# Summing the scan's products by accumulating DMAs instead of GpSimd adds

## The reference

```python
def ffn(x):                                   # H = 512, I = 2048
    h = silu(x @ w_gate) * (x @ w_up)
    return keep_2_largest_of_4(h) @ w_down    # 2:4 sparsity by magnitude

def mamba(x):                                 # E = 1024 channels, N = 16 states
    xn = rmsnorm(x) * norm_w
    skip, u = xn @ W_skip.T, xn @ W_in.T
    u = silu(causal_conv4(u) + conv_b)
    delta = softplus(u @ Wd1.T @ Wd2.T + bd2)
    Bt, Ct, A = u @ WB.T, u @ WC.T, -exp(A_log)
    # for every token l, channel e, state n:
    #   h[e,n] = exp(delta[l,e] * A[e,n]) * h[e,n] + delta[l,e] * u[l,e] * Bt[l,n]
    #   y[l,e] = sum over n of h[e,n] * Ct[l,n]
    return ((y + u * W_D) * silu(skip)) @ W_out.T

x = x + 0.5 * ffn(layernorm(x))
x = x + mamba(layernorm(x))
x = x + 0.5 * ffn(layernorm(x))
```

## Time and profile before

| | |
|---|---|
| median of 3 runs | 4050.57 us (4049.12 to 4053.82) |
| profiled execution | 4051.71 us, its span 4050.0 us |
| PE busy | 3607.4 us (89%) |
| DVE busy | 3205.8 us (79%) |
| POOL busy | 2918.7 us (72%) |
| ACT busy | 2039.0 us (50%) |
| DMA queues of SP and ACT | 37.0% and 12.5% of the sixteen engines' span |

### The profile page before, as it was taken

How to read it: one execution, slowest core, us unless ns; L and a number is a source line. 1 busy time by engine, 2 the same in 40 slices (tenths; PEclk the granted TensorE clock), 3 DMA queues, 4 the chain that set the end, 5 groups by cost and what they waited for, 6 DMA issues and landing times. The chain is left out here.

```text
span 4050.0 us, 38161 instructions
## 1 busy us (share of the span) xinstructions
PE 3607.4 (89%) x11264; PEld 2077.2 (51%) x11264; DVE 3205.8 (79%) x3392; ACT 2039.0 (50%) x2694; POOL 2918.7 (72%) x2249
## 2 busy tenths in 40 slices
PE   7998889999999999899999898899887788787798
PEld 5654555555555555554555454545454344444455
DVE  4425988787989789887999889977988789989823
ACT  3234557547554664557554755466353665353310
POOL 0024789677977899688886998779967989878700
PEclk9999999999999999999999999999898898888899
DMA  6444545544645465354554555546454345444432
GB/s 234 148 134 140 162 147 168 201 148 148 211 159 182 146 202 191 120 187 154 201 172 154 173 164 188 155 139 202 156 171 133 124 148 180 148 126 148 122 123 90
DMA packets 233148, 647.64 MB, mean 160 GB/s; under 512 B 25968, under 2 KB 26224, under 8 KB 223216
## 3 DMA queue, kind: packets, MB, share of 16 engines
q1 hardware_dynamic: 159216, 510.95, 37.0%
q10 hardware_dynamic: 73728, 134.25, 12.5%
HBM read 579.57 MB, written 65.54 MB: 159 GB/s over the span
## 5 line engine op out<-in xcount | busy, mean ns | idle before, releaser
L1096 POOL TENSOR_TENSOR db<-du,Bb 128x512 f32<-128x512 f32 x1024 | 1357.5, 1326 | 539.8 <-DVE decay L990 459.9
L990 DVE TENSOR_TENSOR_SCAN decay<-decay,db 128x512 f32<-128x512 f32 x1024 | 1251.9, 1223 | 268.7 <-ACT decay L690 253.8
L1107 POOL TENSOR_TENSOR y<-y,pr 128x512 f32<-128x512 f32 x1024 | 1382.8, 1350 | 63.9 <-DVE pr L1000 63.9
L690 ACT ACTIVATE decay<-delta,aneg 128x512 f32<-128x512 f32 x1024 | 701.5, 691 | 1187.3 <-DVE pr L1000 1181.1
L523 PE MATMUL main<-zhi,wunit 128*128 128x512 f32 x2048 | 961.4, 469 | 54.4 <-DVE zlo L934 32.5
L582 PE MATMUL side<-h,wdown 128*128 128x512 f32 x2048 | 925.0, 595 | 16.1 <-DVE res_r L975 8.8
L524 PE MATMUL main<-zlo,wunit 128*128 128x512 f32 x2048 | 811.2, 396 | 0.0
L525 PE MATMUL main<-zhi,wunit 128*128 128x512 f32 x2048 | 809.8, 395 | 0.0
L1000 DVE TENSOR_TENSOR pr<-decay,Cb 128x512 f32<-128x512 f32 x1024 | 703.2, 687 | 31.5 <-DVE decay L990 0.3
L582 PEld LDWEIGHTS side<-h,wdown 128*128 128x128 f32 x2048 | 389.0, 190 | 425.6 <-issue 389.1
L598 PE MATMUL side<-xm,wmam 128*128 128x512 f32 x1024 | 488.4, 624 | 60.2 <-ACT cv L771 28.1
(11 more groups left out here) (80 smaller groups left out, 2624.2 us busy)
## 6 DMA issues: line engine op xcount, KB each, us to landing
wunit<-hl_dram SPq DMA_DIRECT2D x480, 512.0 KB, 3.8
wdown<-down_w_dram SPq DMA_DIRECT2D x256, 256.0 KB, 2.9
Bb<-bc_dram ACTq DMA_DIRECT2D x256, 256.0 KB, 3.9
Cb<-bc_dram ACTq DMA_DIRECT2D x256, 256.0 KB, 5.0
wmam<-mam_w_dram SPq DMA_DIRECT2D x64, 512.0 KB, 3.9
hl_dram<-wunit SPq DMA_DIRECT2D x32, 512.0 KB, 2.9
skip_dram<-skb SPq DMA_DIRECT2D x64, 256.0 KB, 4.1
delta<-skip_dram SPq DMA_DIRECT2D x16, 1024.0 KB, 6.6
```

The costliest lines, as they stand in the source:

```text
L690: nc.scalar.activation(decay[u % BANKS][:], delta[:, e, :], ACT.Exp, scale=aneg[:, e, n:n + 1]).then_inc(sem["decay_ready"], 1)
L990: nc.vector.tensor_tensor_scan(decay[u % BANKS][:], decay[u % BANKS][:], db[u % RING][:], 0.0, ALU.mult, ALU.add).then_inc(sem["state_read ...
L1096: nc.gpsimd.tensor_tensor(db[u % RING][:], du[:, e, :], Bb[m % ROWS][:], ALU.mult).then_inc(sem["input_ready"], 1)
L1107: nc.gpsimd.tensor_tensor(y[:, e, :], y[:, e, :], pr[u % RING][:], ALU.add).then_inc(sem["sum_ready"], 1)
```

## The change

The products of two units that follow each other, tiles e and e+1 of one half, go into one buffer `pr[k]` of 128 x 2 x 512, of which there are three. POOL no longer adds them. It issues one DMA for the pair with `accum_op=ADD`, which reads 512 KB of `pr`, adds it to the 512 KB of `y[:, e:e+2, :]` and writes them there. There are 512 such DMAs. Each of the three buffers has a semaphore `summed_k`, which rises by 16 when its DMA has landed. The DMA for pair p waits for that of pair p-2 (same tiles, the state before), DVE waits for pair p-3 before it writes the buffer again, and the gate waits for the last two pairs. The conditions and the plan's tables are otherwise as they were.

```diff
+PAIRS = 3
...
-        pr = [sb(f"pr{k}", [P, L]) for k in range(RING)]
+        pr = [sb(f"pr{k}", [P, 2, L]) for k in range(PAIRS)]
...
+        def wait_sum(eng, p):
+
+            eng.wait_ge(sem[f"summed_{p % PAIRS}"], 16 * (p // PAIRS + 1))
...
-                if u >= RING:
-                    dve.wait_ge(sem["sum_ready"], u - RING + 1)
-                nc.vector.tensor_tensor(pr[u % RING][:], decay[u % BANKS][:], Cb[m % ROWS][:], ALU.mult).then_inc(sem["weighted_ready"], 1)
+                if u % 2 == 0 and u >= 2 * PAIRS:
+                    wait_sum(dve, u // 2 - PAIRS)
+                nc.vector.tensor_tensor(pr[u // 2 % PAIRS][:, u % 2, :], decay[u % BANKS][:], Cb[m % ROWS][:],
+                                        ALU.mult).then_inc(sem["weighted_ready"], 1)
...
-                dve.wait_ge(sem["sum_ready"], UNITS * b + HALF * (half + 1))
+                for p in range(2):
+                    wait_sum(dve, (UNITS * b + HALF * (half + 1)) // 2 - 2 + p)
...
-            def sum_states(u):
-                b, v = divmod(u, UNITS)
+            def sum_states(p):
+
+                b, v = divmod(2 * p, UNITS)
                 half, v = divmod(v, HALF)
                 e = HE * half + v % HE
                 if v == 0:
                     pool.wait_ge(sem["first_term_ready"], HE * (2 * b + half + 1))
-                pool.wait_ge(sem["weighted_ready"], u + 1)
                 if v >= HE:
-                    pool.wait_ge(sem["sum_ready"], u - HE + 1)
-                nc.gpsimd.tensor_tensor(y[:, e, :], y[:, e, :], pr[u % RING][:], ALU.add).then_inc(sem["sum_ready"], 1)
+                    wait_sum(pool, p - HE // 2)
+                pool.wait_ge(sem["weighted_ready"], 2 * p + 2)
+                pool.dma_start(y[:, e:e + 2, :], pr[p % PAIRS][:], accum_op=ALU.add).then_inc(sem[f"summed_{p % PAIRS}"], 16)
...
                 for u in plan.units_at[tick]:
                     scan_input(u)
-                    if u >= RING:
-                        sum_states(u - RING)
+                    if u >= RING and u % 2:
+                        sum_states((u - RING) // 2)
...
-                    for u in range(B * UNITS - RING, B * UNITS):
-                        sum_states(u)
+                    for p in range((B * UNITS - RING) // 2, B * UNITS // 2):
+                        sum_states(p)
```

More of the change, by code:

```diff
@@ L318, in build @@
             "squares_ready", "squares_read", "root_ready", "scaled", "high_part_ready", "normed_ready",
-            "decay_ready", "input_ready", "state_ready", "weighted_ready", "sum_ready",
+            "decay_ready", "input_ready", "state_ready", "weighted_ready",
             "conv_step", "conv_ready", "u_ready", "delta_copied",
@@ L325, in build @@
             "skip_loaded_0", "skip_loaded_1", "bc_stored",
-            *(f"side_read_{k}" for k in range(SIDES)),
+            *(f"side_read_{k}" for k in range(SIDES)), *(f"summed_{k}" for k in range(PAIRS)),
             *(f"b_loaded_{k}" for k in range(ROWS)), *(f"c_loaded_{k}" for k in range(ROWS)),
```

## The result

The changed kernel takes 4392.06 us (median of 4 runs, 4390.72 to 4401.48), the kernel before, on the same chip, 4049.85. The ratio is 1.085, with a 95% interval of 1.0836 to 1.0864: 8.5% slower. The forecast was 4000.

A forecast was written before the change was run, and what follows sets the result against it. No engine was full everywhere: PE set the pace early, DVE late, its two-operand instructions waiting until GpSimd's queued work ran out. 4051.7 - 80 + 5 + 25 = 4001.7, against the median 4000; forecast range 3960 to 4040, wider range 3930 to 4270.

The forecast's parts named there:

- Step 5: Waits of GpSimd and DVE for pair DMAs: landing in 7.5 to 8 us, about the burst's limit; priced at 5 us.
- Step 1: On GpSimd, 1024 adds (1382.8 us) go and each DMA issue takes 1.0 us, so its backlog is gone.
- Step 2: DVE's two-operand instructions get shorter once GpSimd's backlog goes: 150 us back, at least 111, at most about 180.
- Step 3: What reaches the end: 70 us of PE's waits for cmp and zlo, 10 us for convolutions; gain 80, bounds 30 and 150.
- Step 4: Load on the DMA engines: 512 accumulating DMAs at two passes, 2.73 us each, 1398 us; 92% of the scan stretch.
- Step 6: Other transfers get slower: the gate's loads into delta cost DVE 51 us at most, 25 us on the path.
- Rival A: DMA engines become the bound in the scan stretch, at three passes a pair: 4400; chance in full (over 4200) 0.18.
- partial saturation: Bunched traffic fills the DMA engines in some stretches only, costing 50 to 150 us; with rival B, chance 0.25.
- Rival B: Pair DMAs land late, 10 us after issue, so the chain over pairs becomes the wait: 4120; chance with partial saturation 0.25.

The follow-up runs named there:

- e1: The changed kernel with 576 instead of 512 bytes reserved for GpSimd's DMAs: 3998.19 us, ratio 0.9866 to the kernel before.
- e5: The kernel of e2, but GpSimd waits for the landing of pair p-1 instead of p-2, so one DMA is in flight: 4391.47 us, ratio 1.0845.
- e2: The changed kernel with 1024 instead of 512 bytes reserved for GpSimd's DMAs, space won by computing A in place: 3989.75 us, ratio 0.9842.
- e4: The changed kernel, still 512 bytes, with plain copies of the pairs onto y instead of accumulating DMAs: 3892.04 us, ratio 0.9606.
- e9: The kernel of e3 plus one unread product on GpSimd before each scan input, with two pr buffers instead of four: 4055.52 us, ratio 1.0015.
- e3: The kernel before with the sums over the states and the waits for them left out: 3861.98 us, ratio 0.9531.

## Why the prediction failed

**Step 5 failed**, the waits. It took the chain over pairs as the only limit on DMAs in flight, "GpSimd may issue the DMA of pair p only when that of pair p-2 has landed", so two in flight, and priced it at 5 us. In fact one was in flight. Four units in 13.5 us for a landing became two units in 6.8 us. A landing takes 6.4 us in the mean (6.1 in the median), and the next DMA begins 0.3 us after it: the reserve was gone even in the mean, and in a burst two units leave only 3.7 us. The waits went to DVE (397 us before `pr`) and from there to everybody. Priced by e1 against the changed kernel, the step is worth 394 us.

That two pairs are never in flight with 512 bytes and are with 576 is what the landings and e1 show, and that one pair at a time costs this much is what e5 shows. What of those bytes a pair takes, and why a second one fits in 64 more, no run shows; how much room a pair and a copy need was the author's estimate. The trace has 73728 / 512 = 144 packets for each DMA, for copies and accumulations alike, so packets do not tell. What the runs show is idle time ended by "issue" of 1109 us with accumulations in 512 bytes, 30.8 in 576 (e1), 26.5 in 1024 (e2), and 46.5 with copies in 512 (e4).

**Step 1** held: GpSimd's issue takes 0.89 us, I took 1.0, and its backlog went (the longest comparison takes 4.9 us in e2 instead of 10.2). What it missed is that `db` itself got longer, from 1326 ns to 1412 in e2 and 1516 in the changed kernel (1297 in e4, with plain copies); no run says why.

**Step 2** held where two pairs are in flight: 150 us of DVE's 222 (199, and 23 on the gate's products) were to come back. In e2 the four groups take 2022, 1429, 857 and 847 ns, which is 64 x (1668 + 191 + 89 + 348) ns = 147 us, and the gate's products give 64 x (1040 - 711) ns = 21 more. In the changed kernel itself the four groups gave back only 107 us, under the 111 that was to be the least: the 128x512 comparison even rose, from 946 to 1097 ns. e9 shows that GpSimd's instructions alone make the comparisons long, and the rest of the trace of the kernel before bears out the one timeline: of its 22 comparisons of 128x1536 that take over 3 us, 20 end 1.61 to 1.62 us after an unbroken row of 3 to 7 GpSimd instructions; the other two end where GpSimd paused for 79 ns.

**Step 3** was mis-sized. Removing the adds is worth 188 us (e3), not 80; even the upper bound was 150. The step counted PE's named waits for `cmp` and `zlo`, 60% of two thirds of them, and 10 us for the convolutions. In e3 those waits of PE fell by 85 us, more than the 70 counted, and the rest of the gain came by other ways: DVE's busy time fell by 3205.8 - 3005.4 = 200 us, and the end came 188 us earlier. Nor is it only the stretches in which DVE sets the pace: by the start of the fifth sequence's scan e3 is 64 us ahead, by the last scan 187. That each microsecond saved on DVE counted is argued from these numbers, not shown.

**Step 4** held in size: 2.73 us a pair expected, 0.329 x 4388.7 / 512 = 2.82 us in the changed kernel and 2.70 in e2, twice a copy's 1.32 (I had 1.37). So a pair costs two passes, as I took, and not three. The reason that I gave, loads and stores moving at once, has this in the 20 us of the earlier trace rows: a store of `cv` to `u_dram` is issued at 1049.16 us and a load into `wunit` at 1049.53, and such stores land in 3.4 us in the median.

**Step 6** was right for `delta` and too low in all. With room, the DMAs cost 3989.75 - 3861.98 = 128 us of the 188. e4 shows that 30 of them come with plain copies, so 98 with what an accumulation has more: 1.4 us more of the sixteen DMA engines for each pair (2.70 against 1.32), and 0.3 us more of GpSimd for each issue. By the rows of e2 the waits are the expected one for `delta` (53.8 us where it was 5.9; 51 more was the bound, 25 the price), ones that I priced at nothing, PE for `du` (25.0) and `xm` (15.6), and DVE for the pair buffers (45.0, where step 5 had 5).

So e1's 3998 lies on the forecast of 4000, but by luck, two errors that cancel: a gain over twice as large, and a cost of the DMAs over four times as large. **Rival A**, at 4400, has the changed kernel's time and not its cause: a pair costs two passes, not three, the share of the scan stretch is 0.83, and e1, with fuller DMA engines, is 394 us faster. The partial saturation that it named is there, in 18 of 187 stretches of 20 us, and in e1 in 76 of 167; it belongs to what the DMAs still cost there. **Rival B** has the place (waits for the pair's DMA on DVE) and not the cause either; it named late landing, and landings were early, 6.1 us, as only one was in flight (6.0 in e5, which also has one; 8.1 in e2, with up to two).

## What to carry to other kernels

Before giving a stream of DMAs to GpSimd, ask how many fit into the bytes reserved for them, and try a few bytes more: room for one DMA turned a pipeline into a series here, and the profile shows that only as idle time ended by "issue", with each DMA beginning 0.3 us after the landing of the one before. When an engine's time seems to be hidden, compare the durations of the same instructions on its neighbours with and without it at work: here 72% busy and hardly waited for, GpSimd's adds cost 188 us of 4050. And where two engines can both do a job, try to split it: half the pairs by DMA gave 3961 where all by DMA gave 3990 and none 4050, and with the earlier loads, half, alternating, gave 3933 where all gave 3973.

## What was not expected of the hardware

- A reservation of 512 against 576 bytes a partition made 394 us of difference (4392.06 against 3998.19), with every other line of the program the same.
- DVE's instructions with two SBUF operands waited until GpSimd's queued instructions had run out, not for one: up to 10.2 us for a comparison of 1.75, and 20 of the 22 comparisons over 3 us end 1.61 to 1.62 us after an unbroken row of 3 to 7 of them. Taking half of GpSimd's adds away took the mean of the 128x1536 comparison from 3690 to 2179 ns, all of them to 2022.
- A DMA of GpSimd for which there was no room was begun 0.26 to 0.32 us after the landing of the one before, and its own instruction was no longer for it (0.89 us): the wait stands before it, ended by nothing that the profile names.
- Issuing one DMA keeps GpSimd busy for 0.89 us if it accumulates and 0.59 us if it copies (e4), with the same 512 KB.
